# A mixture-of-experts output stage whose two accumulating scatters per tile are issued without a wait between them

## What is computed

```
x = x + _L0_gnn_ref(_layernorm(x), src, dst, edge_weight, W, b)
x = x + _L0_ffn_ref(_layernorm(x)[None], ...)[0]
x = x + _L1_gnn_ref(_layernorm(x), edge_weight1, weight, gate_weight, src, dst, edge_type_16)
x = x + _L1_ffn_ref(_layernorm(x)[None], Wg, bg, W1, b1, W2, b2)[0]
```

```
top_w, top_i = jax.lax.top_k(gate_logits, TOP_K)
top_w = jax.nn.softmax(top_w, axis=-1)
for e in range(E):
    h = jax.nn.gelu(xf @ W1[e] + b1[e], approximate=False)
    out = out + w_dense[:, e:e + 1] * (h @ W2[e] + b2[e])
```

## Time and profile before

| | |
|---|---|
| time, median of 3 runs | 4001.26 us (3999.29 to 4010.76) |
| span of the profiled execution, first to last instruction | 3402.6 us |
| what lies around the span, against the median | 598.7 us |
| prelude, two gathers, table stage, placing | 0 to about 2737 us |
| experts stage | about 2737 us to the end |
| PE busy over the span | 77% |
| POOL busy over the span | 55% |

### The profile page before, as it was taken

One profiled execution on the slowest core, in us unless ns is written; L12 is line 12 of the kernel. 1 busy time (PEld: TensorE's weight loads), 2 busy tenths in 40 slices (PEclk: granted clock), 3 DMA queues, 4 the chain that ended last, 5 costly groups with the idle time before them and its releaser, 6 DMA issues. The chain is left out here.

```text
span 3402.6 us, 59974 instructions
## 1 busy us (share of the span) xinstructions
PE 2615.4 (77%) x14271; PEld 1921.6 (56%) x14272; DVE 1733.1 (51%) x5663; ACT 723.6 (21%) x1907; POOL 1869.7 (55%) x1915
## 2 busy tenths in 40 slices
PE   7688888887777799999655555564555389999997
PEld 6577777776665344444344444443444267767774
DVE  6455545454554655555355454544544544545553
ACT  4121111111110233333211010000000233333332
POOL 1777777777774000000377777777777245555554
PEclk9899999998999899999888888777777689999998
DMA  7333333333332444444545454555544623222232
GB/s 224 110 113 113 113 111 111 113 113 113 110 113 67 173 197 192 188 191 194 194 141 155 151 154 142 152 154 151 146 146 146 241 59 48 45 45 48 45 48 33
DMA packets 175589, 434.08 MB, mean 128 GB/s; under 512 B 41712, under 2 KB 103792, under 8 KB 169232
## 3 DMA queue, kind: packets, MB, share of 16 engines
q0 software_dynamic: 97072, 236.21, 26.9%
q1 hardware_dynamic: 57424, 183.78, 14.1%
q10 hardware_dynamic: 21008, 13.24, 1.3%
HBM read 275.05 MB, written 158.04 MB: 127 GB/s over the span
## 5 line engine op out<-in xcount | busy, mean ns | idle before, releaser
L776 POOL DMA_INDIRECT g_msg<-table,idx x1564 | 1517.3, 970 | 518.8 <-issue 476.5
L848 PE MATMUL psum<-g_msg,g_hot 128*128 x3328 | 967.4, 456 | 593.0 <-SPq L719 358.1
L848 PEld LDWEIGHTS psum<-g_msg,g_hot 128*128 128x128 f32 x3328 | 756.5, 233 | 789.5 <-issue 654.5
L796 DVE TENSOR_SCALAR g_hot<-iota,g_cols 128x128 f32<-128x128 f32 x1664 | 450.1, 364 | 31.9 <-DVE g_cols L793 30.5
L1908 POOL DMA_INDIRECT out<-ex_y,ex_to x112 | 206.0, 1839 | 253.9 <-DMA out<-ex_y,ex_to 165.3
L768 POOL MEMSET g_origin<- 128x256 f32 x1 | 0.3, 313 | 590.8 <-POOLq L1359 590.8
L1594 PE MATMUL psum<-wrel_halves,t_xhi 128*128 128x512 f16 x784 | 298.2, 380 | 1.7 <-DVE t_row L1475 1.7
L1595 PE MATMUL psum<-wrel_halves,t_xhi 128*128 128x512 f16 x784 | 298.1, 380 | 0.0
L1596 PE MATMUL psum<-wrel_halves,t_xlo 128*128 128x512 f16 x784 | 298.1, 380 | 0.0
L1475 DVE TENSOR_SCALAR t_row<-psum,t_gate 128x256 f32<-128x256 f32 x392 | 171.2, 479 | 233.7 <-PE psum L1596 231.7
L2074 PE MATMUL psum<-w,ex_ghi 128*128 x784 | 260.6, 382 | 6.7 <-DVE ex_y L1983 6.4
(11 more groups left out here) (353 smaller groups left out, 3231.7 us busy)
## 6 DMA issues: line engine op xcount, KB each, us to landing
table<-t_row SPq DMA_DIRECT2D x48, 2048.0 KB, 6.3
g_msg<-table,idx POOLq DMA_INDIRECT x1564
piece_stage<-in_w SPq DMA_DIRECT2D x32, 512.0 KB, 5.7
w_halves<-piece_halves SPq DMA_DIRECT2D x32, 512.0 KB, 3.4
w<-w_halves SPq DMA_DIRECT2D x8, 2048.0 KB, 22.6
rows<-sc_row ACTq DMA_DIRECT2D x50, 128.0 KB, 2.2
out<-acc ACTq DMA_DIRECT2D x49, 128.0 KB
table<-t_row SPq DMA_DIRECT2D x24, 256.0 KB, 2.5
```

The lines of the kernel that those rows point to most:

```text
L776: pool.indirect_dma_start(out=msg[:, at:at + D], out_offset=None, in_=table, in_offset=bass.IndirectOffsetOnAxis(ap=t[f"idx{g}"][:, n:n + ...
L796: last = nc.vector.tensor_scalar(hot[b][:, k * P:(k + 1) * P], t["iota32"][:, :], c3[:, k, where:where + 1], c3[:, k, weight:weight + 1], ...
L848: pe.matmul(ps, hot[b % PAIR][:, k * P:(k + 1) * P], msg[:, bass.ds(slot_at[k], D)], start=False, stop=False, skip_group_check=True).then_ ...
```

## The change

Four edits. First, `add` issues the scatters of both halves one after the other; the wait for `added` between them is gone. Second, the spare rows that unused places add to are doubled: an unused place of the first half has a target of its own among 128 rows, one of the second half among 128 others (`behind` has SUBS columns, `out` has 128 more rows, `ex_none` is twice as wide and zeroes both blocks). Third, the number of a slot and of a closed window is read with `value_load`, which checks bounds, in place of a load that skips the check. Fourth, two register values that waits use are masked with `& 1023`.

```diff
     def slot_number(eng, m):
-        _, (n,) = nc.values_load_multi_w_load_instructions(slot_at(m, 0, 1), engines=[eng.engine], min_val=0, max_val=WINDOWS,
-                                                           skip_runtime_bounds_check_because=sure)
-        return n
+        return eng.value_load(slot_at(m, 0, 1), min_val=0, max_val=WINDOWS)
...
-                    pe.wait_ge(tiles_in, code[MSG_TILES])
+                    pe.wait_ge(tiles_in, code[MSG_TILES] & 1023)
...
-                            pe.wait_ge(bank_free, code[BATCH + k // BANKS] + 1)
+                            pe.wait_ge(bank_free, (code[BATCH + k // BANKS] & 1023) + 1)
...
-                    _, (n,) = nc.values_load_multi_w_load_instructions(
-                        t["closed"][0:1, bass.ds(m, 1)], engines=[act.engine], min_val=0, max_val=WINDOWS - 1 - k,
-                        skip_runtime_bounds_check_because=sure)
+                    n = act.value_load(t["closed"][0:1, bass.ds(m, 1)], min_val=0, max_val=WINDOWS - 1 - k)
...
-            "cycle": every(np.arange(cls.CYCLES) * cls.CYCLE * P), "behind": END + p + 1}
+            "cycle": every(np.arange(cls.CYCLES) * cls.CYCLE * P), "behind": END + np.arange(SUBS)[None, :] * P + p + 1}
...
-        chain(nc.vector.tensor_scalar(self.none[:, :], self.node[:, :], 0.0, const["behind"], ALU.is_le, ALU.mult))
+        of_sub = lambda x: x[:, :].rearrange("p (n s) -> p n s", s=SUBS)
+        chain(nc.vector.scalar_tensor_tensor(out=of_sub(self.none), in0=of_sub(self.node), scalar=0.0,
+                                             in1=const["behind"].unsqueeze(1).to_broadcast([P, PLACE_TILES, SUBS]), op0=ALU.is_le, op1=ALU.mult))
...
-    none = w.sb("ex_none", [P, D], F32)
+    none = w.sb("ex_none", [P, SUBS * D], F32)
...
                 for s in range(SUBS):
-
-                    if s:
-                        core.hold(pool, "pool", added, 16 * (SUBS * n + s + 1))
                     pool.indirect_dma_start(out=out, out_offset=bass.IndirectOffsetOnAxis(ap=to[b][:, s:s + 1], axis=0),
                                             in_=y[b % 2][:, s * D:(s + 1) * D], in_offset=None, compute_op=ALU.add).then_inc(added, 16)
...
-            pool.dma_start(out[END:END + P], none[:, :]).then_inc(added, 16)
+            pool.dma_start(out[END:END + TOKENS].rearrange("(s p) d -> p s d", p=P), none[:, :].rearrange("p (s d) -> p s d", d=D)).then_inc(added, 16)
...
-    out = nc.dram_tensor("out", (END + P, D), F32, kind="ExternalOutput").ap()
+    out = nc.dram_tensor("out", (END + TOKENS, D), F32, kind="ExternalOutput").ap()
```

More of the change, by code:

```diff
@@ L1642 @@
     GROUPS = [range(n, min(n + GROUP, WINDOWS)) for n in range(0, WINDOWS, GROUP)]
-    FIELDS = {"number": CYCLE, "index": EXPERTS, "off": PICKS, "within": COLS, "tile_no": PLACE_TILES, "cycle": CYCLES, "behind": 1}
+    FIELDS = {"number": CYCLE, "index": EXPERTS, "off": PICKS, "within": COLS, "tile_no": PLACE_TILES, "cycle": CYCLES, "behind": SUBS}
     WIDTH = sum(FIELDS.values())
```

## The result

The changed kernel takes 4022.39 us (median of 6 runs, 4010.28 to 4034.81), the kernel before 4009.41 us on the same chip (6 runs). The ratio is **1.0045, 95% interval 1.0028 to 1.0062**: slower by 13 us (the two medians) to 18 us (the ratio, which is not the quotient of the medians). The prediction said 3984 us and gave this side 7 in 100. Its sign, its time and its range are all wrong.

What follows compares the result with a forecast made beforehand. It took POOL's gathers to pace the gather stages and PE to nearly bound the experts stage. -14.5 - 4.4 + 0.2 + 0.5 + 2 = -16.2 us took 4001.3 to 3985, stated as 3984, range 3977 to 4002.

Steps and rivals of the forecast that it cites:

- Register work: Gather stages: masks 20 us on PE, checks 20 us per engine, nearly all covered; 0.5 us taken, bounds 0 and 40.
- the 598.7 us around it: Whole kernel: constant time outside the profiled span, added to about 3386 us to give the forecast time.
- The sign of being wrong: Start of the experts stage: starting later by over 5 us would point to rival 3.
- rival 3: Gather stages: register work isn't covered, 20 us of masks and 20 of checks on PE, less 18; about 4022; chance 0.03.
- Loop and end: Experts stage: dropping the wait between scatters wins 14.5 us over 51 periods, and 4.4 us after the last `ex_y`.
- The port allowance of 2 us: Experts stage: 2 us allowed for tiles where an earlier gather delays DVE's `ex_ghi`; bounds 0 and 0.35 us per tile.
- rival 1: Experts stage: gathers hold back DVE's `ex_ghi`, giving back 10 to 18 us, so 3994 to 4001; chance 0.25.
- rival 2: Experts stage: DVE waits out the whole gather, 0.8 us per tile, 42 us against 18 won; about 4025; chance 0.04.
- Rivals 4: Experts stage: PE's idle time isn't from late gathers and stays, so only the end is won; 3997; chance 0.08.
- 5: Experts stage: the second scatter is held up behind the first though no wait is written; 4001; chance 0.05.
- The spare rows: Doubled spare rows: 0.3 us more on POOL, hidden, and 0.1 to 0.2 us more on DVE once; 0.2 in the sum.

Runs made afterwards that it cites:

- e1: The kernel before with the register edits alone (bounds checks, masks on TensorE), scatters and spare rows as before: 4095.73 us, ratio 1.0103 to the kernel before.
- e5: The kernel of e3 with each of TensorE's three masks per batch done twice: 4041.15 us, ratio 1.0086 to the kernel before.
- e3: The changed kernel with the bounds checks of slot numbers and closed windows replaced by one mask each: 4070.88 us, ratio 1.0017 to the kernel before.
- e7: The kernel of e3 with Pool's wait between the two scatters of a tile put back: 4032.56 us, ratio 1.0064 to the kernel before.
- e2: The changed kernel measured once more, beside e1, with nothing altered: 4075.82 us, ratio 1.0046 to the kernel before.
- e8: The kernel of e3 with each gather fetching rows of 128 numbers in place of 256: 4014.32 us, ratio 1.0022 to the kernel before.
- e9: The kernel of e3 with each gather fetching 64 rows in place of 128: 4081.33 us, ratio 1.0098 to the kernel before.
- e4: The changed kernel with TensorE's gather-stage loop holding two batches and one slot, not four and two: 4098.73 us, ratio 1.0095 to the kernel before.

## Why the prediction was wrong

**The step that failed** is "*Register work.* [...] All this lies in the gather stages, where POOL's gathers set the pace and PE waits for tiles. I take 0.5 us for the last batches, where nothing covers it; bounds are 0 and 40 us." The cover that this term rested on did not exist, and where it stands in the sum as 0.5 us, e1 measured 42 us (give or take 10): 28 for the masks of TensorE (e5) and 12 for the checks beyond a mask (e3); the 2 that are left mean nothing, as each part has an error of 8 to 14. Every trace but the one that I had shows Pool waiting 622 to 705 us for the ring, so what delays TensorE there delays the ring and all behind it.

**What I could have seen.** The premise stood in the table of times: a span of 3402.6 us in an execution put at 4001.3. I wrote "the 598.7 us around it" and added it as a constant. Nothing that I had put 598.7 us outside the span. The gap, 15% of the time, should have made me ask whether this trace was that of a timed execution. It was not, as the spans of the 69 timed executions show, so the earlier trace rows could not decide which engine sets the pace. The sign of being wrong that I had named for rival 3, an experts stage that starts over 5 us later, came with 637 us (tile 4's transposes at 3405.93 for 2768.86), but nearly all of that is the difference between the two traces and not the change.

**The size of the register work, taken as 20 us of masks and 20 of checks**, was low per operation and high in exposure. An operation lasts about 36 ns, but the next one follows after some 0.1 us; the first starts of these three lines lie at 92.6, 92.7 and 92.8 us (ns min/median/max, first and last start):

```profile
L839 PEldq ALU_OP  x208: 3/36/700, 92.6 to 3300.7; - x104
L840 PEldq ALU_OP  x208: 5/36/699, 92.7 to 3300.8; - x104
L844 PEldq ALU_OP  x832: 3/36/709, 92.8 to 3301.8; - x167
```

With 0.1 us each the three masks would be 62 us; the path paid 28, a little under half. Perhaps a wait often follows them that would have lasted as long anyway; no run shows that for TensorE. Of the 20 us of checks it paid 12. So rival 3 came true, "20 us of masks and 20 us of checks on PE, less 18", with 42 less 19 to 23, but its size came out by the cancelling of two errors. That its 4022 is also the time measured is luck: it was counted from 4001.3, and the kernel before ran at 4009.41 beside it. Its chance, 0.03, rested on the earlier trace rows alone.

**The scatters were right in each step.** Loop and end were forecast at 14.5 + 4.4 = 18.9 us, and 19 (e7) and 23 us (e1, e2) were measured. The traces of before and after give 15.2 us for the loop (581.81 less 566.64) and 4.5 for the end, those of e1 and e2 15.7 and 4.0. The experts stage can be compared between them, as TensorE's granted clock is 1.00 in the windows of both. The second scatter follows 1.9 us after the first, `ex_y` releases Pool, no transposes wait for gathered rows inside the loop, and PE is busy over 98%.

**The port allowance of 2 us** was not needed: all 56 `ex_ghi` take 1.23 us (before the mean was 1.24 and the longest 1.50), and the gathers pay (mean 2146 ns in place of 1012, 104 gathers each). So rivals 1 and 2 are out. The Trainium skill (SBUF — State Buffer, SBUF: two separate sides) gives the shared port pair to whichever starts first, a GpSimd instruction or one of VectorE that uses the pair, for its whole instruction. The rows disagree for a gather that began first, as far as Pool's rough start times tell: `ex_ghi` started 0.24 us into it, was not held, and the gather took 1.59 us. They agree where VectorE began first: the next gather, started 0.40 us into `ex_glo`, ended 0.87 us after it. Rivals 4 (only the end is won) and 5 (the second scatter is held up) are out by the periods and the 1.9 us.

**The spare rows** were given 0.2 us; no experiment changed them alone. They are in the 23 us by which e1 and e2 differ and not in the 19 of e7, and the traces leave no more than a few us for them.

**Open:** what makes the instructions late. They come late in both gather stages on TensorE, VectorE, ScalarE and SyncE, whose register operations are recorded there at up to 0.7 to 1.4 us. The experts stage has loops too in which TensorE, VectorE and ScalarE load and check registers and jump, and none of those operations takes over 0.33 us in the changed kernel's trace, so loading and jumping alone don't do it. The bytes or rows of the gathers (e8, e9) and the length of TensorE's loop (e4) make no difference; whether the instructions are fetched late for another reason is not tested. The old trace has none of it, and why that one execution was spared I can't say. Nor was the kernel before profiled in an execution like the timed ones: that these are long shows in their spans and their clock, but that its gather stages have this shape is concluded from e7.

## What to carry to other kernels

Set the span of the profiled execution against the measured time before anything else: here 2 us lay between them in every execution but one, and in that one the trace showed another execution than the timed ones, whose bound proved nothing about them. A change with two parts, of which one looks like form only (a check, a mask, a clamp), has two prices; here the harmless-looking one cost 42 us and the other won 20. In a loop over a ring, count register operations on the engine that frees the ring (0.037 to 0.045 us each here, a little under half of their 0.1 us) even where one trace calls them covered, add constants in the table and not in the loop, and put checks where an engine waits anyway.

## What was not expected of the hardware

- In the gather stages of all profiled executions but one, sequencers start instructions late by about 0.7, 1.4, 2.1 or 2.8 us, in the middle of runs of equal matmuls (1.4 to 2.8 us apart from 429.85 to 440.40). The 32 matmuls of line 1064 take 16.0 us there in place of 3.73. Even a register operation with a median of 36 ns is seen at up to 700 ns.
- TensorE's granted clock is lower there. In the stretch from 170 to 680 us it is 0.77 in the mean, against 0.96 in the earlier trace rows. In the first broken group the pauses come first: the granted clock was 0.97 from 139.0 to 149.9 us and 0.67 from there to 159.7. The matmul behind the first pause takes 0.27 us, those behind the next ones 0.37:

```profile
150.57 0.27 PE L1064 MATMUL psum<-f_xT,w 128*128 128x128 f32 x1 [0.68 <-issue]
153.38 0.37 PE L1064 MATMUL psum<-f_xT,w 128*128 128x128 f32 x1 [2.54 <-issue]
```

- A gather of 64 rows takes Pool nearly as long as one of 128: 916 ns in the mean against about 968 (e9). Its cost there is not that of its rows.
- A gather beside VectorE stretches to up to 2.76 us, and a VectorE instruction that starts 0.24 us into one isn't delayed.
